# A fixed order of steps per head group in a hand-scheduled attention stage, with negated row maxima written straight in fp16

## The reference, cut to what matters

```python
n_head = 32; h = C // n_head                       # T = 1024, C = 512, so h = 16
q, k, v = (proj(wq), proj(wk), proj(wv))
q = _apply_rope(q, sin, cos); k = _apply_rope(k, sin, cos)
scores = jnp.einsum('bnth,bnsh->bnts', q, k) * (1.0 / math.sqrt(h))
scores = jnp.where(causal, scores, -jnp.inf)
attn = jax.nn.softmax(scores, axis=-1)
out = jnp.einsum('bnts,bnsh->bnth', attn, v)
```

## Time and profile before

| what | time |
|---|---|
| median of 3 runs | 903.25 us (903.22 to 903.79) |
| the profiled execution, its own time | 899.88 us |
| its span, first to last instruction | 898.2 us |
| projections and searches of group 0, up to | 458 us |
| attention stage, first turn to last out | 458 to 684 us |
| out projection, norm, second feed-forward, norm | 684 to 898 us |

### The profile page before, as it was taken

How to read it: one execution, slowest core, us unless ns; L and a number is a source line. 1 busy time by engine, 2 the same in 40 slices (tenths; PEclk the granted TensorE clock), 3 DMA queues, 4 the chain that set the end, 5 groups by cost and what they waited for, 6 DMA issues and landing times.

```text
span 898.2 us, 19543 instructions
## 1 busy us (share of the span) xinstructions
PE 820.1 (91%) x8137; PEld 383.1 (43%) x8137; DVE 645.6 (72%) x912; ACT 438.4 (49%) x578; POOL 305.6 (34%) x219
## 2 busy tenths in 40 slices
PE   7669788887999999999979999999987999999997
PEld 2434344434444444455533444334423444444443
DVE  4999999985565334444678999999956878776334
ACT  4976566536654311344435666767676243333100
POOL 0799899992000011254430122111222312331000
PEclk9599898997999999999978999999999899999999
DMA  7800000004240000000000000000022113330011
GB/s 229 336 2 3 3 3 3 3 3 163 94 112 1 1 1 0 1 1 1 1 1 2 2 1 2 2 2 1 2 80 94 58 58 114 115 114 0 4 44 47
DMA packets 21937, 38.25 MB, mean 43 GB/s; under 512 B 6993, under 2 KB 12881, under 8 KB 21858
## 3 DMA queue, kind: packets, MB, share of 16 engines
q1 hardware_dynamic: 21858, 37.11, 12.3%
HBM read 34.87 MB, written 2.16 MB: 41 GB/s over the span
## 4 chain that ended last, share of the span: by engine, by line
PE 70%; DVE 16%; issue 6%; POOL 4%; ACT 2%; SPq 1%; DMA 1%; DVEq 0%; POOLq 0%; ACTq 0%
PE ps L864 13%; PE ps L664 11%; PE ps L641 9%; PE ps L891 6%; DVE arena L1543 6%; PE ps L815 6%; PE ps L715 5%; DVE arena L1344 5%; PE ps L751 5%; POOL arena L1196 3%; PE ps L799 3%; PE ps L514 2%; PE ps L558 2%; PE ps L728 2%; PE ps L755 2%
## 5 line engine op out<-in xcount | busy, mean ns | idle before, releaser
L1543 DVE TENSOR_REDUCE arena<-ps 128x1 f32<-128x512 f32 (+3 forms) x320 | 183.8, 630 | 18.1 <-PE ps L755 12.5
L1134 ACT ACTIVATE arena<-ps 128x1024 f32<-128x1024 f32 (+2 forms) x160 | 144.2, 942 | 75.1 <-PE ps L799 74.8
L1196 POOL TENSOR_TENSOR arena<-arena 128x1024 f32<-128x1024 f32 x64 | 158.6, 2516 | 9.7 <-DVE arena L1344 9.2
L1344 DVE TENSOR_TENSOR_SCAN arena<-arena,ps 128x1024 f32<-128x1024 f32 x64 | 142.1, 2270 | 1.8 <-PE ps L558 1.4
L864 PE MATMUL ps<-arena 128*128 128x512 f16 x528 | 114.3, 379 | 1.6 <-DVE arena L1433 1.6
L1245 POOL TENSOR_SCALAR_AFFINE_SELECT arena<-arena 128x512 f32<-128x512 f32 x64 | 40.6, 634 | 182.8 <-ACT arena L1134 182.8
L664 PE MATMUL ps<-arena 128*128 128x512 f16 x448 | 97.5, 379 | 1.7 <-DVE arena L1474 1.7
L751 PE MATMUL ps<-arena 64*128 64x512 f16 (+3 forms) x384 | 97.5, 342 | 0.7 <-DVE arena L1543 0.7
L979 ACT ACTIVATE arena<-arena,negA 128x1024 f32<-128x1024 f32 x64 | 73.0, 1146 | 48.1 <-DVE arena L1344 45.9
L641 PE MATMUL ps<-arena 128*128 128x512 f16 x384 | 89.5, 387 | 5.0 <-DVE arena L1407 3.3
L558 PE MATMUL ps<-arena 64*128 64x64 f16 x3072 | 61.4, 197 | 34.7 <-DVE arena L1344 31.5
(11 more groups left out here) (155 smaller groups left out, 971.0 us busy)
## 6 DMA issues: line engine op xcount, KB each, us to landing
arena<-in_w_q_dram SPq DMA_DIRECT2D x11, 768.0 KB, 4.4
arena<-c_rows SPq DMA_DIRECT2D x16, 512.0 KB, 11.1
arena<-in_w_s_dram SPq DMA_DIRECT2D x11, 384.0 KB, 4.6
arena<-in_x_fm_dram SPq DMA_DIRECT2D x8, 256.0 KB, 4.1
out_dram<-arena SPq DMA_DIRECT2D x8, 256.0 KB, 2.0
arena<-in_wg_dram SPq DMA_DIRECT2D x1, 1792.0 KB, 9.6
arena<-in_wu_dram SPq DMA_DIRECT2D x1, 1792.0 KB, 7.4
arena<-in_wd_dram SPq DMA_DIRECT2D x1, 1792.0 KB, 10.5
```

The costliest lines, as they stand in the source:

```text
L1134: nc.scalar.activation(dst, src, ACT.Exp, scale=float(HD) ** -0.5).then_inc(exp_done, 1)
L1196: nc.gpsimd.tensor_tensor(hC[i % 4][:], hst[i % 3][:], c_all[:, n, :], ALU.mult).then_inc(hc_done, 1)
L1344: nc.vector.tensor_tensor_scan(hst[i % 3][:], dA[i % 3][:], banks(2 * (i % 2), 2), 0.0, ALU.mult, ALU.add).then_inc(scan_done, 1)
L1543: nc.vector.reduce_max(maxima_slot(half, k), ps[:, ring_bank(n), 0:len(heads) * w].rearrange("p (a w) -> p a w", a=len(heads)), AX).then_i ...
```

## The change

The planner goes. In its place stands one string of 78 letters, a period, that is repeated for each group; START says which step of its kind a letter of period 0 begins with (s: search number 32 of a group, so that a period begins at search 20 of half 1; k: one unit back; v: three tiles back, and so on). Steps of groups that do not exist, and the early searches, are skipped. The counts of searches, keys, values, turns and outs are the same as before. Second, `reduce_max` writes its result negated, for tiles i of the lower bank of keys directly into m_neg, in fp16; m_a is gone and m_b is fp16. The multiplication by -1 is gone for both halves. For half 0 nothing is left on DVE at the letter n; for half 1 one `min` of m_neg[1] and m_b is left, with no wait behind it on DVE. PE's turn of half 0 waits for the last search's read, the turn of half 1 for the join.

```diff
-        m_a = view(199, TT * GH, f32).rearrange("p (i a) -> p i a", i=TT)
-        m_b = view(199.25, 4 * GH, f32).rearrange("p (i a) -> p i a", i=4)
+        m_b = view(199.25, 4 * GH, f16).rearrange("p (i a) -> p i a", i=4)
...
-            dst = m_b[:, i - 4, :] if key else m_a[:, i, :]
+            dst = m_b[:, i - 4, :] if key else m_neg[i // 4][:, i % 4, :]
...
-        TURN_AFTER = 2
-        VALUES_LAG = 2
         RING = 3
+        PATTERN = ("sskskvkssvsvsskknovsstksssvsksskssksksv"
+                   "svsnkkssvtsskskssvsksokssvsksksvssksksv")
+        START = {'s': 32, 'k': -1, 't': 1, 'o': -1, 'v': -3, 'n': 1}
         def attention_order():
...
+            order = []
+            for period in range(-2, NG + 2):
+                taken = dict.fromkeys(of_group, 0)
+                for letter in PATTERN:
+                    steps = of_group[letter]
+                    g, at = divmod(period * len(steps) + START[letter] + taken[letter], len(steps))
+                    taken[letter] += 1
+                    kind, half, *rest = steps[at]
+                    if not 0 <= g < NG or (kind == "search" and g == 0 and (half, *rest) in EARLY_UNITS):
+                        continue
+                    order.append((kind, g, half, *rest))
+                    if kind == "values" and rest[0] == 4 * half + 3:
+                        order.append(("keep", g, half))
             return order
...
             def turn_maxima(g, half, n):
-                pe.wait_ge(m_negated, 2 * g + half + 1)
+                if half:
+                    pe.wait_ge(m_joined, g + 1)
+                else:
+                    pe.wait_ge(ring_read, RING_AT.get(("search", g, 0, len(SEARCH[0]) - 1), EARLY - 1) + 1)
...
-                                     AX).then_inc(ring_read, 1)
+                                     AX, negate=True).then_inc(ring_read, 1)
...
             def negate(g, half):
-                last = RING_AT.get(("search", g, half, len(SEARCH[half]) - 1), EARLY - 1)
-                dve.wait_ge(ring_read, last + 1)
                 if half:
-                    nc.vector.tensor_tensor(m_a[:, 4:TT, :], m_a[:, 4:TT, :], m_b[:], ALU.max).then_inc(m_joined, 1)
-                    dve.wait_ge(m_joined, g + 1)
-                nc.vector.tensor_scalar(m_neg[half][:], m_a[:, 4 * half:4 * half + 4, :], -1.0, None, ALU.mult).then_inc(m_negated, 1)
+                    dve.wait_ge(ring_read, RING_AT["search", g, 1, len(SEARCH[1]) - 1] + 1)
+                    nc.vector.tensor_tensor(m_neg[1][:], m_neg[1][:], m_b[:], ALU.min).then_inc(m_joined, 1)
```

More of the change, by code:

```diff
@@ L178, in build @@
         v_ringed, ring_full, ring_read = sem("v_ringed"), sem("ring_full"), sem("ring_read")
-        m_joined, m_negated, r_made = sem("m_joined"), sem("m_negated"), sem("r_made")
+        m_joined, r_made = sem("m_joined"), sem("r_made")
         m_rows = [sem("m_rows0"), sem("m_rows1")]
@@ L232, in build @@
         MASK_TO = list(itertools.accumulate(int(on_diagonal(half, j)) for _, half, j in STEPS))
-        TURN_AFTER = 2
-        VALUES_LAG = 2
         RING = 3
+        PATTERN = ("sskskvkssvsvsskknovsstksssvsksskssksksv"
+                   "svsnkkssvtsskskssvsksokssvsksksvssksksv")
+        START = {'s': 32, 'k': -1, 't': 1, 'o': -1, 'v': -3, 'n': 1}
         def attention_order():
[L240 to L298, removed]
-                            kept[(step[1], 1) if step[2] == 0 else (step[1] + 1, 0)] = act
-                            outs.append((act, "out", step[1], step[2]))
-                            order.append(("keep", step[1], step[2]))
-                    continue
-                if which == 1:
-                    step = outs.pop(0)[1:]
-                    pe, cost = at + 0.1 + 0.55, 0.55
-                else:
-                    step = side.pop(0)
-                    pe, cost = at + 0.05 + 0.35, 0.55
-                    if step[0] == "search":
-                        i, key, w, heads = SEARCH[step[2]][step[3]]
-                        pe = at + 0.05 + len(heads) * (w * 0.6 * col + (0.06 if key + w == P * (i + 1) else 0.0))
-                        cost = 0.07 + len(heads) * w * 1.04e-3
-                order.append(step)
-                dve = max(dve, pe + fill + hop) + cost
-                ring.append(dve)
-                if step[0] == "turn":
-                    rows[step[1:]] = dve + 2.6
@@ new lines, in attention_order @@
+            of_group = {
+                "k": [("keys", half, j, u) for half in range(2) for j in range(4 * half + 4) for u in exp_units(half, j)],
+                "v": [("values", half, j) for half in range(2) for j in range(4 * half + 4)],
+                "s": [("search", half, k) for half in range(2) for k in range(len(SEARCH[half]))],
+                "n": [("negate", half) for half in range(2)],
+                "t": [("turn", half) for half in range(2)],
+                "o": [("out", half) for half in range(2)]}
```

## The result

The changed kernel takes 911.29 us in the median of four runs (905.53 to 917.86) against 903.24 before: the ratio is 1.010, with a 95% interval of 1.0064 to 1.0136. Run again beside two experiments it came to 915.07 us, 1.013 (1.0085 to 1.0175). It is 1.0 to 1.3% slower, where 0.6% faster was forecast. The profiled execution took 910.71 us with a span of 909.0.

A forecast was written before the change was run, and what follows sets the result against it. DVE was taken to set the attention stage's pace. Saving 0.65 us per group over seven periods gives 4.6 us, plus 0.8 in the head, tail nothing: 5.4 us, median 903.25 to 897.8, range 890 to 908.

The forecast's parts named there:

- Part 1: Negation inside DVE's reduction removes multiplications and a wait: 0.20 us saved for half 0, 0.40 us per group in all.
- Sum per group: 24.8 - 0.4: DVE's own time per group, 24.4 us after the negation's saving; with 2.1 us of stalls a period of 26.5 against 27.16.
- The row wait: Keys j = 0 of half 1 wait for the maxima's rows; DVE stands 1.27 us before search 8 in each group.
- The other stalls: DVE's stalls on PE per group: 0.17 at half 0's turn, 0.36 before search 20, 0.1 before 16, 0.2 small ones.
- the path from copy to keys: From the turn's copy on DVE over SP's four DMAs to the keys on PE: 3.58 us.
- The tail: After the last search the copy ends 2.1 us after the last reduction's start, as before (2.0); same DMAs and exponentials: nothing.
- the head: In group 0 DVE's 0.88 us stand for the first rows mostly goes, as the keys come behind search 22: 0.8 us saved.
- the clock rival: PE idles some 1.4 us in one piece per group and the clock falls: period 28.6 us, time 912; chance 0.08.
- Stalls only change places: Long bursts on PE find the ring not full; one more stall like the old 0.76 per group: 903 to 904; chance 0.15.
- The row wait is covered: The copy comes earlier or the other gaps were overestimated: period 25.6 to 25.9, typically 893; chance 0.20.
- The slower reduction: DVE's reduction with negation costs more: 0.02 us each gives 903, 0.08 gives 920; chance 0.07.

The follow-up runs named there:

- order_only: The changed kernel with the old f32 maxima and the multiplication by -1 back in, four DMAs per turn: 913.39 us, 1.0135 of the kernel before.
- order_two: The new order with the old f32 maxima and multiplications, and two DMAs per turn in place of four: 892.73 us, 0.9887 of the kernel before.
- after: The changed kernel itself, new order and negation in the reduction, four DMAs per turn, against the kernel before: 911.29 us, 1.010.
- two_dmas: The changed kernel with two DMAs of two rows each per turn in place of four of one row: 891.29 us, 0.9884 of the kernel before.
- filler: The changed kernel with four dummy matmuls before the keys that wait for the rows of half 1: 904.95 us, 1.001 of the kernel before.
- after_again: The changed kernel run once more, unchanged, beside two experiments on one chip: 915.07 us, 1.013 of the kernel before.
- neg_only: The changed kernel with the old planner back in, so old order with negation in the reduction: 900.50 us, 0.9986 of the kernel before.
- keys_later: The changed kernel with the two key units that begin half 1 moved behind two more searches: 915.14 us, 1.0118 of the kernel before.

## Why the prediction was wrong

**Part 1** held for the old order: 0.40 us per group, no more than 2 ns per reduction for the sign and the fp16 result, and the gap behind a wait (0.11 us dearer) is real. It failed in the step that carried this gain over to the new order, "Sum per group: 24.8 - 0.4": that sum is of DVE's time, and DVE does not set the pace of the new order (4% of the chain of work). The periods of order_only and order_two against after and two_dmas show that the 0.40 us are worth 0.00 to 0.02.

**The row wait** was found and well sized: 1.27 us forecast, 1.13 seen as idle, 1.21 with the lost overlap; the keys 3.6 us after the copy. **The other stalls** were too small: 0.54 for 0.36 ahead of search 20, 0.28 for none ahead of search 0 (the burst k k n o v is not quite covered), 0.15 behind the copy and some small ones. Undisturbed periods are 27.09 for 26.5, so 4.1 us of the 4.6 forecast were not there.

**The step that turned the sign** is the treatment of the path from copy to keys as one number, 3.58 us. The trace of before already had issues of 0.97 and 1.23 us among the 0.59s and landings up to 2.8 us at a median of 1.7; they were harmless there because 4.4 us were allowed. Once the path is exposed, each late DMA counts in full, and behind the longest holes the clock falls. Against 27.09 the disturbed periods cost 2.01 + 0.22 + 0.68 + 3.18 = 6.1 us. Of these 2.9 are the late rows themselves (1.01 + 0.21 + 0.67 + 1.04), and the other 3.2 came in the two periods with the low clock, which the sum had at nothing. The tail, with 2.53 us of empty PE and the low clock behind it, costs 2.6 us more. It was put at nothing too: the copy does end at the same distance, but the keys' wait there grew from 1.12 us to 2.53, as the out and the values of 512 queries that filled it are done earlier now. Even with seven undisturbed periods, then, the stage would have gained next to nothing: -1.2 for the periods, -0.7 for the head, +2.6 for the tail. (The -1.2 counts the last period at 27.09 as well. In filler it is 26.86 with keys 0.69 us late, so undisturbed it is nearer to 26.2, which makes it -2.2, and the last period's fall of the clock dearer by 0.9.)

The stage by its sum: periods -4.6 forecast, +4.9 measured (195.7 against 190.9: seven of 27.09 would be 189.6, 1.2 less than before, and the disturbed ones add the 6.1); head -0.8 forecast, -0.7 measured; tail 0 and +2.6. The rest of the 10.8 us between the two profiles, 4 us, lies ahead of the stage and is the spread of executions.

**The rivals**: the clock rival had the place right and half of the mechanism, and its 912 is what came out. That the number fits is partly luck: it had every period at 28.6 us, where in the trace three of seven are undisturbed and two have the clock's fall behind late rows, of which it said nothing; and 4 us of the difference between the profiles are not of the stage. Its low chance of 0.08 was argued from a wait of 1.81 us that left the clock at 1.00. But that is the idle time of the weight loads; the matmuls stood only 1.12 us there, less than the 1.4 us expected in each group, so the row could not speak against the rival:

```profile
666.58 0.39 PE L799 MATMUL ps<-arena 64*128 64x512 f16 x2 [1.12 <-DMA arena<-arena]
```

"Stalls only change places" was half true: undisturbed periods gained 0.07 us, but the row wait and not the bursts took the rest. "The row wait is covered", 893, is what a shorter path gives (891.3). The slower reduction is out, at 2 ns.

**Two small sums** of the prediction don't add up, and nothing hangs on them: DVE's own time per group is 24.1 + 0.20 + 0.43 = 24.7 us, not 24.8, and the chances as listed give faster 0.62 and same 0.14, not 0.64 and 0.12.

## What to carry to other kernels

When an order is packed more tightly, look for the longest latency that it now leaves without slack, and cost that path with its worst instances in the trace, not its median: above all several small DMAs issued one behind the other. Here one edit to that path, two DMAs in place of four, is worth 5 to 20 us, turns a loss of 1% into a gain of 1.2% (of which 0.5% is what it gives the kernel before by itself) and works in either order. And before carrying a gain on one engine into a new schedule, ask whether that engine still sets the pace there; one period that is the same to 0.02 us in kernels with different work says that it does not, and so does its small share of the chain of work.

## What the runs showed of the hardware

- A one-row DMA from SP takes 0.59 us to issue, but in each profile with four of them per turn two to seven of the 64 take 0.8 to 1.9 us, and during each of these a packet of the instruction queue runs (after: 503.94 and 642.95 us; before: 564.74). A DMA of two rows takes no longer: 1.16 us for two of them, and none of 160 took over 0.71.
- With all four issues regular a row can still land late: 3.44 us after its issue in after_again and 3.61 in neg_only, where the median is 1.7.
- A reduction that writes negated fp16 takes 684 ns for 512 inputs in the old order (neg_only) where the plain f32 one takes 682, and 686 in the new order (after) where the plain one takes 684 (order_only).
- The clock falls to 0.50 for 3.4 to 6.8 us at a time in the changed kernel (10.2 once in keys_later) behind some holes of PE and not behind others of nearly the same length (filler, above).
